# Attention scores as three passes over high and low halves, in a decoder layer with hand-ordered engine lists

## The reference

```python
x = _layernorm(x + attn(x))          # causal self-attention, 16 heads of 64, 8 groups of keys and values
x = _layernorm(x + xattn(x, ctx))    # cross-attention to 77 context rows, 8 heads of 64
x = _layernorm(x + ffn(x))           # gated, 256 -> 768 -> 256, integer weights scaled by 1/127
```

```python
q = einsum('bsd,dhe->bshe', x, W_Q); k = einsum('bsd,dge->bsge', x, W_K); v = einsum('bsd,dge->bsge', x, W_V)
scores = einsum('bqgre,bkge->bgrqk', q, k) / sqrt(64)      # two query heads r share the keys of group g
probs  = softmax(where(later key, -1e6, scores))
out    = einsum('bshe,ehd->bsd', einsum('bgrqk,bkge->bqgre', probs, v), W_out) + b_out
```

## Time and profile before

| | |
|---|---|
| median of 3 runs | 2188.42 us (2185.69 to 2190.17) |
| profiled execution | 2187.84 us |
| its span, first to last instruction | 2186.0 us |
| mean granted TensorE clock | 0.992 |
| busy: TensorE, its weight loads | 2121.0 us, 1864.6 us |
| busy: VectorE, ScalarE, GpSimd | 1574.8 us, 1331.5 us, 393.2 us |

### The profile page before, as it was taken

How to read it: one execution, slowest core, us unless ns; L and a number is a source line. 1 busy time by engine, 2 the same in 40 slices (tenths; PEclk the granted TensorE clock), 3 DMA queues, 4 the chain that set the end, 5 groups by cost and what they waited for, 6 DMA issues and landing times.

```text
span 2186.0 us, 55834 instructions
## 1 busy us (share of the span) xinstructions
PE 2121.0 (97%) x18368; PEld 1864.6 (85%) x18368; DVE 1574.8 (72%) x5700; ACT 1331.5 (61%) x3990; POOL 393.2 (18%) x630
## 2 busy tenths in 40 slices
PE   4899999999999999999999999999999999999986
PEld 3688888888888888888888888888888888888875
DVE  3477777777777777777777777777777777777764
ACT  5666666656666656666656666656666656666642
POOL 3211121111112111112111112111112111112111
PEclk9899999999999999999999999999999999999998
DMA  4100000000000000000000000000000000000000
GB/s 133 41 14 15 15 8 17 17 17 11 16 8 17 17 17 10 17 8 17 17 17 10 17 8 17 17 17 10 17 8 17 17 17 10 17 8 17 14 6 10
DMA packets 48599, 38.47 MB, mean 18 GB/s; under 512 B 19504, under 2 KB 46512, under 8 KB 48560
## 3 DMA queue, kind: packets, MB, share of 16 engines
q1 hardware_dynamic: 48560, 37.96, 6.1%
HBM read 29.56 MB, written 8.39 MB: 17 GB/s over the span
## 4 chain that ended last, share of the span: by engine, by line
PE 95%; DVE 1%; ACT 1%; DMA 1%; POOL 1%; issue 1%; SPq 0%; POOLq 0%; DVEq 0%; ACTq 0%
PE gen L375 21%; PE gen L377 18%; PE gen L376 18%; PE s_ps L509 10%; PE z_ps L543 7%; PE pt_ps L522 3%; PE gen L439 3%; PE gen L457 3%; PE gen L470 3%; PE z_ps L545 3%; PE pt_ps L523 3%; PE pt_ps L527 2%; PE gen L466 2%; PE gen L481 1%; PE gen L434 1%
## 5 line engine op out<-in xcount | busy, mean ns | idle before, releaser
L679 ACT ACTIVATE SM<-SM,least 128x128 f32<-128x128 f32 (+1 forms) x1024 | 452.9, 446 | 142.0 <-DVE least L975 141.9
L975 DVE CUSTOM_DVE_ANT_0 SM<-s_ps,causal 128x128 f32<-128x128 f32 (+1 forms) x1024 | 312.5, 352 | 111.3 <-PE s_ps L509 105.6
L615 ACT ACTIVATE PT<-pt_ps 128x512 f32<-128x512 f32 (+1 forms) x512 | 237.7, 485 | 207.8 <-PE pt_ps L523 161.5
L988 DVE TENSOR_SCALAR SM<-SM,total 128x128 f32<-128x128 f32 (+1 forms) x1024 | 274.5, 332 | 9.1
L1157 POOL TENSOR_TENSOR H_lo<-G,H_hi 128x256 fp32r<-128x256 f32 x192 | 142.1, 753 | 620.7 <-ACT H_hi L615 620.7
L509 PE MATMUL s_ps<-KT,QT 64*128 64x128 f32 (+1 forms) x2048 | 238.5, 351 | 4.3 <-DVE least L975 3.5
L1133 POOL TENSOR_TENSOR var<-moments,eps 128x2 f32<-128x2 f32 x96 | 18.7, 195 | 1054.3 <-DVE moments L847 1054.3
L679 ACT ACTIVATION_READ_ACCUMULATOR SM<-SM,least 128x1 f32 x1024 | 195.3, 191 | 0.0
L543 PE MATMUL z_ps<-PT,Vt 128*64 128x256 f32 x1024 | 170.4, 407 | 6.2 <-ACT PT L615 6.2
L509 PEld LDWEIGHTS s_ps<-KT,QT 64*128 64x128 f32 x2048 | 135.0, 187 | 43.2 <-issue 28.6
L984 DVE RECIPROCAL total<-total 128x4 f32<-128x4 f32 x256 | 44.4, 173 | 163.6 <-ACT SM L679 159.3
(11 more groups left out here) (176 smaller groups left out, 6611.8 us busy)
## 6 DMA issues: line engine op xcount, KB each, us to landing
xT_in<-in_xT SPq DMA_DIRECT2D x32, 256.0 KB, 2.8
x_in<-in_x SPq DMA_DIRECT2D x32, 256.0 KB, 2.8
out<-XN SPq DMA_DIRECT2D x32, 256.0 KB, 2.2
ctx_in<-in_ctxT SPq DMA_DIRECT2D x32, 77.0 KB, 2.4
mask_in<-in_maskT SPq DMA_DIRECT2D x32, 77.0 KB, 2.6
QX<-in_wq SPq DMA_DIRECT2D x1, 512.0 KB, 4.6
QP<-in_wq SPq DMA_DIRECT2D x1, 512.0 KB, 5.4
xwk<-in_xwkv SPq DMA_DIRECT2D x1, 512.0 KB, 5.5
```

The source lines that it names most:

```text
L615: return act.activation(o, i, ACT.Copy)
L679: ins = act.activation(part, part, ACT.Exp, scale=-1.0, bias=least[:, i % 2, n:n + 1], accum_out=total[:, i % 2, n:n + 1])
L975: ins = dve.tensor_tensor_reduce(SM[:, i % 2, at:at + keys], s_ps[h][:, t * P:t * P + keys], causal[:, S - keys:S], -SCALE, -3 * NEG, ALU. ...
L988: ins = dve.tensor_scalar(part, part, total[:, i % 2, n:n + 1], None, ALU.mult)
```

## The change

The queries and keys are kept as halves, and a score product is three matmuls of 64 rows in place of one plain float32 product. ScalarE copies a Q or K bank into the high half and no longer frees the bank; VectorE gets a new step that subtracts the high half from the bank, writes the low half and frees the bank. Two signals, `q_high` and `k_high`, tie the two. The lists of items and of every engine but SyncE are written in another order. One argument of the program's constructor sets the size of a scratch area for transfers.

```diff
-        QT = sb("QT", [P, 2, 2, S])
-        KT = sb("KT", [P, NJ, S])
+        QT_s = halves("QT", [P, 2, 2, S])
+        KT_s = halves("KT", [P, NJ, S])
...
+        q_high = signal("q_high", NP // 2)
+        k_high = signal("k_high", NJ // 2)
...
                     for t in range(T):
                         keys = P * (t + 1)
-                        for h in range(2):
-                            rows = slice(h * E, (h + 1) * E)
-                            ins = pe.matmul(s_ps[h][:, t * P:t * P + keys], q[rows, t * P:(t + 1) * P],
-                                            KT[rows, i // 2, 0:keys], start=True, stop=True)
+                        for n, (left, right) in enumerate(((0, 0), (0, 1), (1, 0))):
+                            for h in range(2):
+                                rows = slice(h * E, (h + 1) * E)
+                                ins = pe.matmul(s_ps[h][:, t * P:t * P + keys], q[left][rows, t * P:(t + 1) * P],
+                                                k[right][rows, 0:keys], start=(n == 0), stop=(n == 2))
...
                     if kind[0] == "Q":
-                        copy(QT[:, c % 2, :, :], halves_view(ps[:, :])).then_inc(read_out, 1)
+                        copy(QT_s[0][:, c % 2, :, :], halves_view(ps[:, :])).then_inc(q_high.sem, 1)
...
+                    if kind[0] in "QK":
+                        batch = b + 1 if name[0] == "n" else b
+                        if kind[0] == "Q":
+                            dve.wait_ge(q_high.sem, q_high.at(batch, c + 1))
+                            high, low = [part[:, c % 2, :, :] for part in QT_s]
...
+                        dve.tensor_tensor(low, two, high.bitcast(F32), ALU.subtract).then_inc(read_out, 1)
...
+                   dynamic_dma_scratch_size=4096)
```

More of the change, by code:

```diff
@@ L496, in scores @@
                         return
-                    q = QT[:, i // 2 % 2, i % 2, :]
+                    q = [part[:, i // 2 % 2, i % 2, :] for part in QT_s]
+                    k = [part[:, i // 2, :] for part in KT_s]
                     if i == 0:
@@ L547, in values @@
                     ins.then_inc(z_full.sem, 1)
+                fill("aQ1")
+                scores(0)
+                fill("fXOUT")
+                transposed("o", 7)
                 fill("oXK")
[L550 to L553, removed]
+                scores(1)
                 values("o", 7)
-                scores(1)
+                transposed("a", 0)
+                fill("aV1")
+                scores(2)
                 fill("aV0")
                 fill("oOUT0")
-                transposed("a", 0)
+                fill("fT3")
+                values("a", 0)
                 fill("oOUT1")
-                fill("fT3")
-                scores(2)
-                fill("aV1")
+                transposed("a", 1)
+                scores(3)
                 fill("fFFN0")
@@ L565, in body @@
                 fill("aK1")
-                scores(3)
-                transposed("a", 1)
+                fill("aQ2")
                 fill("fFFN2")
-                values("a", 0)
-                fill("aQ2")
+                transposed("a", 2)
+                values("a", 1)
                 fill("oT10")
                 fill("oT11")
-                transposed("a", 2)
                 scores(4)
@@ L585, in body @@
                 fill("aQ3")
+                values("a", 3)
+                transposed("a", 4)
                 fill("oSIM10")
-                values("a", 3)
+                fill("nQ0")
+                fill("nK0")
                 scores(6)
-                transposed("a", 4)
+                values("a", 4)
+                fill("oT201")
                 fill("fDOWN1")
+                fill("oT200")
+                transposed("a", 5)
                 fill("oXV")
-                transposed("a", 5)
-                values("a", 4)
-                fill("nK0")
+                values("a", 5)
                 scores(7)
[L596 to L599, removed]
                 fill("fDOWN0")
-                transposed("a", 6)
                 fill("oT210")
                 fill("oT211")
+                transposed("a", 6)
                 fill("oXPV0")
@@ L1203, in body @@
                 gated_low(3)
+                late()
+                x_low()
                 gated_low(4)
                 gated_low(5)
-                late()
-                x_low()
                 deviation_3()
```

148 lines of the change are left out of this document (78 added, 70 removed), and 4 rows, old and new, of the table ITEMS.

## The result

The changed kernel takes 2205.48 us (median of 4 runs, 2204.27 to 2207.87) beside 2189.3 us for the kernel before (4 runs, 2185.69 to 2191.41): ratio 1.0077, 95% interval 1.006 to 1.0094. So it is slower by 16.2 us. The forecast was 2195 us, slower by 6.6.

A forecast was written before the change was run, and what follows sets the result against it. TensorE, without slack in the steady state, was taken as the bound: 2187.84 + 8.7 (scores calls) - 3.1 (order) + 1 (start and end) = 2194.4, with 0.58 to the median 2195 us. Range 2183 to 2226 us.

The forecast's parts named there:

- The scores call: TensorE's score products: six pairs at weight-load or stream pace make a call 0.894 us, 0.034 us more than before.
- rival 1: Scores call: weight loads hide behind streams, so a call takes 0.69 us; -43.5 us in place of +8.7; 6 in 100.
- The term of +8.7 us: Cost of the scores in halves over the whole program: 256 calls, each 0.034 us longer.
- Rivals 2 and 3: Scores call: 2, slow short streams (+84 us, 8 in 100); 3, halves one after another (+170 us, 4 in 100).
- The order: TensorE's list: two more layout entries begin with transposes, saving 0.10 us a turn, -3.1 us over 31 turns.
- rival 4: Steady turn: TensorE waits once or twice, each 0.5 us a turn costing 15.5 us; 13 in 100.
- The tightest slack: Steady turn: nQ0, moved next to the split of the next batch's x, has 0.35 us to spare.
- the six subtractions: VectorE's new work on Q and K: 4.1 us a batch, hidden while TensorE has other work queued.
- Start and end: Sparse stretches before and after the steady state: +1 us, between -6 and +6.
- GpSimd's late split: GpSimd's list: moved with x_low ahead of the last two gated_low, with 12 us of work in a turn.
- rival 5: The new list shortens start and end by more than the products cost; 2184 at 10 us won; 9 in 100.

The follow-up runs named there:

- experiment 4: Changed kernel, but the first query tile's score products also run over all 256 keys: 2209.04 us, ratio 1.009.
- experiment 5: Changed kernel without the product of high queries and low keys, so two passes in place of three: 2151.87 us, ratio 0.9834.
- experiment 1: Changed kernel's new lists with the plain products, copies and waits of the kernel before: 2194.53 us, ratio 1.0019.
- 9: Plain products; new lists in the loop with values(0), values(1), values(3) moved next to score products (three joins), old lists in the first two turns: 2169.71 us.
- experiment 2: Kernel before with the scores in halves, their copies and subtractions, all in the old lists: 2211.61 us, ratio 1.0098.
- experiment 10: Changed kernel with three values products moved next to score products in the loop (joins), old lists in the first two turns: 2179.82 us, ratio 0.9956.
- experiment 3: Changed kernel, but in the first turn alone nQ0 and nK0 come behind transposed(5): 2199.61 us, ratio 1.0047.
- 6: Changed kernel with the old lists in its first two turns and the new ones from there on: 2196.81 us, ratio 1.0038.
- 7: Kernel before with values(0), values(1) and values(4) moved next to score products (three joins), to avoid layout changes: 2187.61 us, ratio 0.9996.
- 8: Kernel before with two joins: values(0) ahead of transposed(1), nK0 ahead of values(4); values(1) not moved: 2183.0 us, ratio 0.9974.

## Why the prediction was right in direction and short in size

**The scores call: right.** 0.894 us forecast, 0.885 measured, 0.856 before. Pairs over 128 keys take 0.11 us, the pace that the forecast took for their weight loads, whatever they stream (experiments 4 and 5). That rules out rival 1 (0.69 us a call). The Trainium skill (TensorE: Matmul & The Clock Gate, LDWEIGHTS) names this pace: by its rule a load of 128 columns takes an estimated 0.107 us, and the trace agrees with its 0.11. The term of +8.7 us was 256 x 0.029 = 7.4.

**Rivals 2 and 3: no.** A short stream in halves isn't slow and the two heads' halves run side by side; either would have shown in the six rows of the call.

**The order: the term was mis-sized.** Forecast -0.10 us a turn from more entries that begin with transposes; experiment 1 measured -0.19. It wasn't split by entry. The joins show that an entry avoided is worth 0.16 to 0.19 us where nothing else becomes late (two joins: 0.23, with 0.14 lost again elsewhere; experiments 1 and 9: three joins, 0.49).

**No new wait in the loop (rival 4): right.** TensorE is busy for 1842.00 of 1842.00 us, and no wait for another engine stands in its rows there. The tightest slack, nQ0 behind the split of x, was worked out as 0.35 us; in a turn of the changed kernel `xTs_lo` is done at 1046.23 and nQ0 starts at 1046.70, 0.47 us later. The others weren't measured. Experiment 2 shows what the rival would have looked like: one wait of 0.40 us in each of the 28 turns, and 0.35 us more a turn than the halves cost in the new lists. The turn was forecast as 65.9 us and is 65.79, being 65.70 - 0.19 + 0.28. VectorE has 51.1 us a turn against 53.2 forecast. In one plan the six subtractions add 3.3 us of busy time and not 4.1 (experiments 9 and 10: 1437.67 - 1344.20, by 28), and the new plan has less of it by itself.

**Start and end: the step that failed.** "I take +1 us, between -6 and +6." The first two turns took 11.4 us more, the end 3.7, together 15.1, 9 us outside the bounds of the term. That the total of 2205 us still lies well inside the range of 2183 to 2226 is luck: the range reached that far for a new wait in the loop (rival 4), which didn't come, while the forecast's own terms ended at 2206, and as likely at 2204. The causes, as far as the runs show them:

- The first turn, +6.2 us: 4.2 of them go when nQ0 and nK0 stand late there (experiment 3), all when the old list does (6). The prediction had found this place, nQ0 with the split of x, as the tightest, but worked it out for the steady turn; of GpSimd's late split it said only that there are 12 us of work in a turn. In the first turn `late` has a weight to split: 1.81 us behind a transfer, a conversion and a copy. The halves themselves cost little there: 0.4 us in the old lists (experiment 2 against the kernel before), 2.7 in experiment 10 against 9, both no more than two executions can differ by.
- The second turn, +5.2: the lists alone give 3.2 (experiment 1), the halves in the old lists 1.6 (2). The changed kernel waits there for the normalised x, 1.28 us at T10's products and 1.77 us at XQ0 (before: 1.31 us at XQ0 alone). TensorE runs at the lower level in the first 4.8 us of the turn (a clock of 0.50 from 84.32 to 89.10), behind the gaps of the first, and again behind the wait at XQ0. Of the 5.2 us, 1.0 is idle time (5.25 against 4.30) and 4.2 is busy time, of which the eight calls explain 0.2; most of the rest is the clock, 0.93 against 1.00. With the lists alone (1) the idle time is 4.46 us and the clock 0.95, so there too the lists cost by the clock and not by idle time. Which move of the lists does it wasn't tested.
- The end, +3.7: not the change, as far as these runs tell. Experiment 2 has the lists of the kernel before, no scores left in that stretch, the same 464 matmuls and nearly the same waits, and takes 87.5 us too. Its busy time is 4.5 us longer, with a clock of 0.85 against 0.91. Experiments 7 and 8 have plain products and the same 464 matmuls there, and take 90 us at 0.84. The idle time is 25.0 to 26.3 us in all twelve kernels, so the end follows the clock, and the profiled execution of the kernel before had the best one. Why some executions lose the clock there and others don't stays open.

Since the lists account for most of the loss at the start, rival 5 named the right place with the wrong sign.

## What to carry to other kernels

Price an exchange of product kinds by the longer of weight load and stream, pass by pass: here the 128-key part of a call grew from 0.33 to 0.39 us and the 256-key part shrank from 0.53 to 0.49 (with their layout changes), where a count of columns promised a quarter off both. Where a list is planned for the steady turn, walk it once more for each written-out turn, with what the helpers do only there (here a weight split in front of the one input that was moved up); an order that is free in the loop cost 6 us in one turn. And when a move is meant to save a fixed cost, look first at which bank or operand it makes due earlier: three moves that were meant to save 0.2 us each gave nothing together, and 6 us with one of them taken back.

## What the runs showed of the hardware

The granted clock depends on the program and on more than it. The kernel before ran 46 times beside the experiments: its mean clock lay between 0.989 and 0.994 and its time between 2183.99 and 2193.37 us. The four executions of the changed kernel had 0.986 to 0.988, so its lower clock is not one profile's chance. What it looks like inside: two kernels reach the context keys at the end by the same wait of 1.65 us and with the same instructions. TensorE's timeline, the kernel before, then experiment 2:

```profile
2102.59 2.01 PE L439 MATMUL gen<-ctx_in,xwk 128*128 128x77 f32 x16 [1.65 <-DVE H_lo L938]
2104.44 0.27 PE L522 MATMUL pt_ps<-ident,SM 128*128 128x128 f32 x1
...
2105.34 0.28 PE L377 MATMUL gen<-xwo_hi,H_lo 128*128 128x256 f32 x1
2105.46 0.28 PE L375 MATMUL gen<-xwo_hi,H_hi 128*128 128x256 f32 x1
```

```profile
2123.60 3.34 PE L441 MATMUL gen<-ctx_in,xwk 128*128 128x77 f32 x16 [1.65 <-DVE H_lo L951]
2126.73 0.42 PE L526 MATMUL pt_ps<-ident,SM 128*128 128x128 f32 x1
...
2128.44 0.41 PE L379 MATMUL gen<-xwo_hi,H_lo 128*128 128x256 f32 x1
2128.65 0.41 PE L377 MATMUL gen<-xwo_hi,H_hi 128*128 128x256 f32 x1
```

The one goes on at 2.4 GHz, 0.12 us a product, the other at 1.2 GHz, 0.21 us. The same happens in the first turn of the changed kernel, where the first 22 products behind the wait of 3.9 us take 4.87 us in place of 22 x 0.118 = 2.6. The window:

```profile
67.06:71.93 4.87, 4.87 (x23) 4.87 (x24) 0.69 (x1) 0.60 (x1) 1.19 (x1) 0.50 0.19 54
```

The clock is 0.50 throughout (the count of 23 takes in the product that starts at its edge). So a wait in a stretch with gaps costs its own length and, in some executions, a few microseconds at the lower level behind it. A term of start and end that is read from busy time and waits alone is uncertain by that much here: 4 us, more than the change's whole effect on the loop.

The second thing is how flat the price of a pair over 128 or 256 columns is: twice the columns made it 0.007 us dearer (experiment 4), while leaving a pair out gave back 0.113 us (experiment 5).
